# Counting edges per bucket: column sums of one-hots, moved from VectorE to TensorE

## The chip, the cores and the metric

The kernel runs on one core of a Trainium2 chip. The metric is the device time of one execution in microseconds (us). A core has five engines that run their own instruction streams and meet at semaphores: TensorE (PE in the rows; its weight loads are shown apart as PEld), VectorE (DVE), ScalarE (ACT), GpSimd (POOL) and SyncE (SP), which here only issues transfers.

## The reference

Four layers follow one another on 8192 rows of 128 numbers, each added to its input: a dense attention over an adjacency matrix, an expert layer whose gates come from a graph attention over 524288 edges, a second dense attention, and a routed expert layer. The change lies in the preparation of the edges for the second layer, which needs, for each destination node, sums over the edges that lead to it:

```python
src = jnp.concatenate([edge_index[0], loops])
dst = jnp.concatenate([edge_index[1], loops])
e = jax.nn.leaky_relu(a_src[src] + a_dst[dst], negative_slope=0.2)
e_max = jax.ops.segment_max(e, dst, num_segments=M)
ee = jnp.exp(e - e_max[dst])
denom = jax.ops.segment_sum(ee, dst, num_segments=M)
alpha = ee / (denom[dst] + 1e-16)
agg = jax.ops.segment_sum(h[src] * alpha[:, :, None], dst, num_segments=M)
```

## The kernel before

Edges lie as 128 partitions by CE = 4096 columns. Edges into the last row with a source beyond it ("same") are only counted; the others whose both ends lie in the 8192 rows are "plain" and get sorted into NF = 64 buckets, one for each tile of 128 destination nodes.

The function sort_and_project has two phases. In "pack" VectorE squeezes the plain edges of each partition to the left, so that only some hundred columns are left, and writes to ctl how many groups of GB = 64 columns the fullest partition needs. In "bucket" each plain edge gets its place: its rank among all edges of its bucket. Each phase ends in a barrier of all engines.

The bucket phase, by engine, in program order:

- GpSimd makes tile_no (the bucket numbers 0 to 63, each repeated 64 times) and keep, clears a column of recs, and then stores packed pieces of the adjacency.
- VectorE first **counts**: for each group it compares tile_no with the group's bucket numbers partB (L788, a one-hot tile of 64 buckets by 64 columns), sums the one-hot over its columns (L793, into some) and adds that to held (L794). Then it signals held_ok and waits for base_ok. It copies BASE into column 0 of D1 (L800), takes the largest total (L801) and derives from it the number of rounds and of fills (L802 to L807). Then it **places**: for each group a one-hot, a scan along the columns, a product, a reduction over the buckets (L818), eight small steps and a signal to SyncE to store the group's part of the plan. At last it makes one-hots for the same edges (L920, L921) and copies the histogram (L836).
- TensorE packs the adjacency: for every tile of 128 rows by 1024 words that ScalarE loads, eight matmuls with 8 columns (L857). Tiles come in units of four, in a ring of eight buffers (NRB); FIRST = 5 units are packed before the counts are wanted, the other 25 after them. Between the two stand two fp32 matmuls on held (L863, L864): one with tri (how many edges of a bucket lie in earlier partitions) and one with ones (how many the bucket has in all). After the packing TensorE counts the same edges in pairs of strided one-hots (L870, closed by L872).
- ScalarE issues the loads of the adjacency tiles, each when a buffer has been eaten, and copies each packed unit out of PSUM (L750).
- SyncE loads H, waits for rounds_ok, fills rec with empty records, and stores each placed group of the plan.

The order on each engine is the order of its program; nothing is planned by cost.

Of the kernel before, what the change touches and what calls it, by code (L numbers as in the profile page):

```python
# [8 lines left out]
ALU = mybir.AluOpType  # L9
ACT = mybir.ActivationFunctionType  # L10
AX = mybir.AxisListType
F32 = mybir.dt.float32
BF16 = mybir.dt.bfloat16
# [5 lines left out]
P = 128  # L19
BANK = 512  # L20
# [219 lines left out]
def sort_and_project(nc, ident, edge_index, N, rec, plan, ctl, repeat, classes,  # L240
# [4 lines left out]
    CE = E // P  # L245
    NF = N // P
    GB = 64
# [10 lines left out]
    with Phase(nc, "sort") as ph:  # L258
# [3 lines left out]
        tri = ph.sbuf("tri", [P, P])  # L262
        ones = ph.sbuf("ones", [P, P])
# [4 lines left out]
        with Phase(nc, "pack") as pk:  # L268
# [6 lines left out]
            plain = pk.sbuf("plain", [P, CE], BF16)  # L275
            S = [pk.sbuf(f"S{k}", [P, CE], I32) for k in range(2)]
            t1 = pk.sbuf("t1", [P, CE])
            scr = pk.sbuf("scr", [P, 6])
            cntc = pk.sbuf("cntc", [P, 2])
            top2 = pk.sbuf("top2", [P, 1])  # L280
            scri = pk.sbuf("scri", [P, 4], I32)
# [26 lines left out]
            groups = [(q, 0, EARLY) for q in range(BLOCKS)] + [(0, EARLY, 3), (0, EARLY + 3, KB - EARLY - 3)]  # L308
# [39 lines left out]
            with nc.Block() as block:  # L348
# [55 lines left out]
                def _(dve):  # L404
# [132 lines left out]
                    step(nc.vector.tensor_reduce(scr[0:1, 5:6], PS[0:1, 2 * P:3 * P], AX.X, ALU.max))  # L537
                    groups_of(0, scr[0:1, 4:5], 2 * GC, 2 * GC + 1.0)
                    groups_of(2, scr[0:1, 4:5], GB)
                    groups_of(3, scr[0:1, 5:6], GC)  # L540
                    step(nc.vector.tensor_scalar(ctl[0:1, 3:4], ctl[0:1, 3:4], float(HELD // GC), 1.0, ALU.subtract, ALU.max))

# [136 lines left out]
        with Phase(nc, "bucket") as pb:  # L679
# [4 lines left out]
            keep = pb.sbuf("keep", [P, NF, GB + 1], BF16)  # L684
            D1 = pb.sbuf("D1", [P, NF, GB + 1])
            ST = pb.sbuf("ST", [P, NF, GB + 1])
            hot = ST[:].rearrange("p t c -> p (t c)").bitcast(BF16)[:, 0:NF * GB].rearrange("p (t c) -> p t c", t=NF)
            some = pb.sbuf("some", [P, NF])
            held = pb.sbuf("held", [P, NF])
            most = pb.sbuf("most", [P, 2])  # L690
            mosti = pb.sbuf("mosti", [P, 2], I32)
            rank = pb.sbuf("rank", [P, GB])
# [12 lines left out]
            pk_out = [pb.sem(f"pk_out{k}") for k in range(2)]  # L705
            HC = CE // 2
            HISTC = pb.psum("histc", [P, BANK])
            BASE = pb.psum("base", [P, 2, BANK])
            same_hot, same_counted, same_ok, zero_ok, made, cleared, empty_ok, dve_step, held_ok, base_ok, rounds_ok, placed = pb.sems(
                "same_hot", "same_counted", "same_ok", "zero_ok", "made", "cleared", "empty_ok", "dve_step", "held_ok", "base_ok", "rounds_ok", "placed")  # L710
            fill_out, plan_out, pool_step, rows_in, passed, classes_out = pb.sems(
                "fill_out", "plan_out", "pool_step", "rows_in", "passed", "classes_out")
            COUNT, EDGE = 3, 13
            slots = rec.rearrange("(p c) k -> p c k", p=P)
            with nc.Block() as block:
                @block.gpsimd
# [61 lines left out]
                @block.vector  # L778
                def _(dve):
                    same_groups = dve.value_load(ctl[0:1, 3:4], min_val=1, max_val=(HC - HELD) // GC)  # L780
                    groups = dve.value_load(ctl[0:1, 2:3], min_val=1, max_val=CE // GB)
                    nc.vector.memset(zero[:], 0.0).then_inc(zero_ok, 1)
                    step = LoopSteps(dve, dve_step)
                    step.now(nc.vector.memset(held[:], 0.0))
                    dve.wait_ge(made, 2)

                    def hots(out, i):
                        return nc.vector.tensor_tensor(out, tile_no[:], partB[:, bass.ds(i * GB, GB)].unsqueeze(1).to_broadcast([P, NF, GB]), ALU.is_equal)  # L788

                    with dve.Fori(0, groups) as i:  # L790
                        step = LoopSteps(dve, dve_step, 1 + i * COUNT)
                        step.now(hots(hot, i))
                        step.now(nc.vector.tensor_reduce(some[:], hot, AX.X, ALU.add))  # L793
                        step.now(nc.vector.tensor_tensor(held[:], held[:], some[:], ALU.add))  # L794
                        assert step.n == COUNT
                    dve.sem_inc(held_ok, 1)
                    first = dve.snap(groups * COUNT + 1)
                    step = LoopSteps(dve, dve_step, first)
                    dve.wait_ge(base_ok, 1)
                    step.now(nc.vector.tensor_copy(D1[:, :, 0], BASE[:, 0, 0:NF]))  # L800
                    step.now(nc.vector.tensor_reduce(most[:, 0:1], BASE[:, 1, 0:NF], AX.X, ALU.max))  # L801
                    step.now(nc.vector.tensor_scalar(most[:, 1:2], most[:, 0:1], float(P * LEAST), float(P - 1), ALU.max, ALU.add))  # L802
                    step.now(nc.vector.tensor_copy(mosti[:, 0:1], most[:, 1:2]))
                    step.now(nc.vector.tensor_scalar(ctl[0:1, 1:2], mosti[0:1, 0:1], LOGP, None, ALU.arith_shift_right))
                    step.now(nc.vector.tensor_scalar(mosti[0:1, 1:2], ctl[0:1, 1:2], float(FILL - 1), None, ALU.add))
                    step.now(nc.vector.tensor_scalar(ctl[0:1, 4:5], mosti[0:1, 1:2], FILL.bit_length() - 1, None, ALU.arith_shift_right))
                    step.now(nc.vector.tensor_scalar(ctl[0:1, 5:6], ctl[0:1, 1:2], -1.0, None, ALU.add))  # L807
                    dve.sem_inc(rounds_ok, 1)
                    dve.wait_ge(cleared, 1)
                    with dve.Fori(0, groups) as i:  # L810
                        step = LoopSteps(dve, dve_step, first + 8 + i * EDGE)
                        cols = bass.ds(i * GB, GB)
                        step.now(hots(D1[:, :, 1:GB + 1], i))
                        step.now(nc.vector.tensor_tensor_scan(ST[:].rearrange("p t c -> p (t c)"), keep[:].rearrange("p t c -> p (t c)"),
                                                              D1[:].rearrange("p t c -> p (t c)"), 0.0, ALU.mult, ALU.add))
                        step.now(nc.vector.tensor_copy(D1[:, :, 0], ST[:, :, GB]))
                        step.now(nc.vector.tensor_tensor(ST[:, :, 1:GB + 1], ST[:, :, 1:GB + 1], D1[:, :, 1:GB + 1], ALU.mult))
                        step.now(nc.vector.tensor_reduce(rank[:], ST[:, :, 1:GB + 1].rearrange("p t c -> p c t"), AX.X, ALU.add))  # L818
                        step.now(nc.vector.tensor_scalar(ri[:, 0, :], rank[:], -1.0, 0.0, ALU.add, ALU.max))
                        dve.sem_inc(passed, 1)  # L820
                        step.now(nc.vector.tensor_copy(ri[:, 1, :], partB[:, cols]))
                        step.now(nc.vector.tensor_scalar(ri[:, 2, :], ri[:, 0, :], P - 1, LOGC, ALU.bitwise_and, ALU.logical_shift_left))
                        step.now(nc.vector.tensor_scalar(ri[:, 3, :], ri[:, 0, :], LOGP, LOGF, ALU.logical_shift_right, ALU.logical_shift_left))
                        step.now(nc.vector.tensor_tensor(ri[:, 2, :], ri[:, 2, :], ri[:, 3, :], ALU.bitwise_or))
                        step.now(nc.vector.tensor_scalar(ri[:, 3, :], ri[:, 1, :], LOGF, 28, ALU.logical_shift_right, ALU.logical_shift_left))
                        step.now(nc.vector.tensor_tensor(ri[:, 2, :], ri[:, 2, :], ri[:, 1, :], ALU.bitwise_or))
                        step.now(nc.vector.tensor_tensor(recs[:, cols, 2], ri[:, 2, :], ri[:, 3, :], ALU.bitwise_or))
                        dve.sem_inc(placed, 1)
                        assert step.n == EDGE
                    with dve.Fori(0, same_groups) as i:  # L830
                        for b in range(2):
                            dve.wait_ge(same_counted, 2 * i + b + 1)
                            cols = bass.ds(i * GC + b * HC + HELD, GC)
                            one_hots_across(nc, OFC[b], OPC[b], value, offC[:, cols], partC[:, cols], NF, GC)[1].then_inc(same_hot, 1)
                    dve.wait_ge(same_ok, 1)
                    nc.vector.tensor_copy(repeat[:], HISTC[:, 0:NF]).then_inc(held_ok, 1)  # L836
                    dve.wait_ge(held_ok, 2)
                    dve.wait_ge(rows_in, 16)
                    nc.vector.memset(H[:, :, D - 1], 1.0).then_inc(held_ok, 1)
                    dve.wait_ge(held_ok, 3)  # L840

                @block.tensor
                def _(pe):
# [4 lines left out]
                    def pack(some):  # L848
                        for u in some:
                            if u >= 2:  # L850
                                pe.wait_ge(emptied, u - 1)
                            for t in range(RT):
# [5 lines left out]
                                                           start=True, stop=True)  # L858
                                ins.then_inc(eaten, 1)

                    pack(range(FIRST))
                    pe.wait_ge(held_ok, 1)
                    nc.tensor.matmul(BASE[:, 0, 0:NF], tri[:], held[:], start=True, stop=True)  # L863
                    nc.tensor.matmul(BASE[:, 1, 0:NF], ones[:], held[:], start=True, stop=True).then_inc(base_ok, 1)  # L864
                    pack(range(FIRST, UNITS))
                    with pe.Fori(0, same_groups) as i:
                        for b in range(2):
# [2127 lines left out]
```

## Time and profile before

| | us |
|---|---|
| median of 3 runs (3690.57 to 3706.22) | 3698.13 |
| the profiled execution: its time | 3702.64 |
| the profiled execution: its span, first to last instruction | 3701.0 |
| TensorE busy, matmuls (16350) | 2732.4 |
| TensorE busy, weight loads (16350) | 1679.7 |
| VectorE busy | 2369.3 |
| ScalarE busy | 1369.6 |
| GpSimd busy | 1087.6 |

The busy times are sums over the whole span, over stages with different limits. The span is what the rows below count time in, from its start; the profiled execution takes 1.6 us more than its span. The bucket phase lies between about 411 and 606 us.

### The profile page before, as it was taken

To read this page: it belongs to the slowest core of one execution; us is meant where nothing else is said; L and a number is where in the kernel's file an instruction comes from. 1 tells how busy PE (TensorE), PEld (TensorE's weight loads), DVE (VectorE), ACT (ScalarE), POOL (GpSimd) and SP (SyncE) were. 2 spreads that over 40 slices of the span, in tenths; PEclk is the share of its full clock that TensorE was granted. 3 is DMA by queue.
4 is the path that set the end of the run, shared out by engine and by line. 5 is a ranking of instruction groups with operands and counts; after the bars stand their busy time and mean duration, and the time that the engine had idled before them with its cause. 6 is when DMAs were issued, how large, how long until landed. Compare 5 with 4: busy or idle time off the path is not lost. (4 is left out here: it accounts for less than half of the span.)

```text
span 3701.0 us, 55128 instructions
## 1 busy us (share of the span) xinstructions
PE 2732.4 (74%) x16350; PEld 1679.7 (45%) x16350; DVE 2369.3 (64%) x4532; ACT 1369.6 (37%) x2278; POOL 1087.6 (29%) x1035
## 2 busy tenths in 40 slices
PE   0442123999999999955888785246999999949994
PEld 0332122444444444424665564244655555526662
DVE  9999797787888878776444446794444444433333
ACT  5310100777777878753344341033000000012221
POOL 0000103777773000001655565000111111114442
PEclk9999999999999999975898895557999999969997
DMA  5999895554545445431111111342333333324446
GB/s 194 355 368 410 321 396 192 182 198 176 187 175 196 186 174 201 158 100 29 43 45 42 42 42 16 104 161 81 104 104 103 108 108 103 108 70 124 126 122 195
DMA packets 233854, 568.88 MB, mean 154 GB/s; under 512 B 52113, under 2 KB 93944, under 8 KB 225134
## 3 DMA queue, kind: packets, MB, share of 16 engines
q1 hardware_dynamic: 146006, 376.34, 29.7%
q10 hardware_dynamic: 56152, 163.80, 11.8%
q0 software_dynamic: 31552, 27.13, 3.3%
q8 instruction: 51, 0.84, 0.1%
q14 instruction: 93, 0.76, 0.1%
HBM read 443.12 MB, written 125.87 MB: 154 GB/s over the span
## 5 line engine op out<-in xcount | busy, mean ns | idle before, releaser
L1881 PE MATMUL at_out<-at_pt,top_H 128*128 128x512 f32 x2048 | 931.7, 601 | 34.8 <-ACT at_agg L1733 29.8
L1723 ACT ACTIVATE at_rl<-at_qrow,at_less,at_steep 128x512 f32<-128x512 f32 x1024 | 741.5, 804 | 89.6 <-DVE at_pt L1809 49.6
L1809 DVE SCALAR_TENSOR_TENSOR at_pt<-at_rl,at_turned 128x1024 f32<-128x1024 f32 x512 | 626.2, 1223 | 157.2 <-PE at_out L1881 80.7
L2098 PE MATMUL at_out<-at_parts,at_a 128*128 128x387 bf16 x4096 | 689.3, 328 | 28.8 <-DVE at_parts L2171 15.7
L1881 PEld LDWEIGHTS at_out<-at_pt,top_H 128*128 128x128 f32 x2048 | 373.0, 190 | 439.2 <-issue 396.6
L2098 PEld LDWEIGHTS at_out<-at_parts,at_a 128*128 128x128 fp8e4 x4096 | 399.4, 98 | 305.6 <-issue 36.8
L903 POOL DMA_INDIRECT rec<-at_part x304 | 384.2, 1264 | 104.9 <-issue 93.2
L1161 POOL DMA_INDIRECT edges_GT<-tab,gat_RC x320 | 339.9, 1062 | 237.0 <-DMA edges_GT<-tab,gat_RC 153.0
L2046 POOL DMA_INDIRECT slots<-at_Y,at_dest x128 | 123.2, 962 | 650.7 <-DVEq L2276 614.6
L648 PE MATMUL pack_bp<-top_weights,sort_recs 128*128 128x8 bf16 x1696 | 76.0, 170 | 233.4 <-DMA sort_recs<-in_adj_dram 233.4
L2549 PE MATMUL ex_hp<-ex_XS,ex_WB 128*128 128x512 f32 (+1 forms) x472 | 217.7, 598 | 1.9 <-DMA ex_WB<-wts 1.9
L2655 POOL DMA_INDIRECT y<-ex_YS,ex_to x156 | 153.3, 983 | 200.3 <-DVE ex_YS L2636 158.8
L2133 ACT ACTIVATE at_small<-at_small 128x4 f32<-128x4 f32 x16 | 3.3, 205 | 517.9 <-DVEq L2229 517.9
L2615 DVE TENSOR_TENSOR ex_HH<-ex_SU,ex_hp 128x512 f32<-128x512 f32 (+1 forms) x118 | 80.9, 686 | 162.8 <-ACT ex_SU L2593 133.3
L648 PEld LDWEIGHTS pack_bp<-top_weights,sort_recs 128*128 128x128 fp8e4 x1696 | 62.0, 106 | 248.7 <-DMA sort_recs<-in_adj_dram 140.8
L1142 POOL IOTA edges_node_no<- 128x128 f32 x1 | 0.2, 237 | 579.3 <-POOLq L63 579.3
L1408 PE MATMUL edges_hp<-top_H,edges_up 128*128 x256 | 150.2, 717 | 19.9 <-issue 17.3
L2593 ACT ACTIVATE ex_SU<-ex_hp 128x512 f32<-128x512 f32 (+1 forms) x118 | 70.3, 596 | 235.7 <-PE ex_hp L2549 192.0
L1800 DVE TENSOR_SCALAR at_turned<-at_packed 128x512 uint16<-128x512 uint16 x520 | 147.9, 286 | 0.0
L1419 PEld LDWEIGHTS edges_yp<-edges_down,f_YB 128*128 128x128 f32 x1024 | 139.5, 211 | 18.6 <-issue 15.9
L1455 PE MATMUL edges_lk<-f_YB 128*128 128x64 bf16 x928 | 119.4, 301 | 30.0 <-DVE f_YB L921 20.3
L857 PE MATMUL bucket_bp<-top_weights,bucket_raw 128*128 128x8 bf16 x960 | 43.9, 170 | 126.9 <-DMA bucket_raw<-in_adj_dram 126.9
(551 smaller groups left out, 3695.4 us busy)
## 6 DMA issues: line engine op xcount, KB each, us to landing
sort_recs<-in_adj_dram SPq DMA_DIRECT2D x212, 512.0 KB, 8.9
at_adj<-in_adj_dram SPq DMA_DIRECT2D x192, 512.0 KB
adjT<-at_turned ACTq DMA_DIRECT2D x64, 1024.0 KB
at_a<-adjT SPq DMA_DIRECT2D x128, 512.0 KB
bucket_raw<-in_adj_dram ACTq DMA_DIRECT2D x120, 512.0 KB, 10.2
ex_WB<-wts SPq DMA_DIRECT2D x42, 533.0 KB
y<-f_YB ACTq DMA_DIRECT2D x64, 256.0 KB
f_YB<-y SPq DMA_DIRECT2D x16, 1024.0 KB, 10.4
```

Of the source, the lines that this page charges most:

```text
L648: ins = nc.tensor.matmul(BP[:, u % 2, o:o + WORDS // 4], raw_bits[s % NR][:, k * P:(k + 1) * P, 0], weights[:], start=True, stop=True)
L903: pool.indirect_dma_start(rec, bass.IndirectOffsetOnAxis(ap=part[h][:, c, 2:3], axis=0), part[h][:, c, 0:2], None, bounds_check=LAST, oob_ ...
L1161: pool.indirect_dma_start(GT[g][:, c, :], None, tab, bass.IndirectOffsetOnAxis(ap=RC[g][:, c, 1:2], axis=0)).then_inc(gt_in[g], 16)
L1408: nc.tensor.matmul(HP[:, k, :], up[:, e, k * P:(k + 1) * P], XT[:, bass.ds(slab[0] * GQ, GQ), :], start=True, stop=True).then_inc(h_ok, 1)
L1419: ins = nc.tensor.matmul(YP[:, q * D:(q + 1) * D], HH[e % 2][k][:, q * P:(q + 1) * P], down[:, e, k, :], start=False, stop=(q == GQ - 1 an ...
L1723: ins = nc.scalar.activation(RL[v % NBUF][:, k, :], qrow[:], ACT.Relu, bias=less[:], scale=steep[:, u:u + 1])
L1800: ins = nc.vector.tensor_scalar(planes[m % 2][:, :, :, b, :], PK[:, m * JP:(m + 1) * JP, :].rearrange("p j (t w) -> p j t w", t=RT), b, 0x ...
L1809: nc.vector.scalar_tensor_tensor(out=PT[v % NBUF][:], in0=RL[v % NBUF][:], scalar=1.0, in1=AT[v // VP % 2][:, 2 * (v % VP):2 * (v % VP) + ...
L1881: ins = nc.tensor.matmul(OUT[:], H[:, u, :], PT[v % NBUF][:, k, :], start=(u == 0), stop=(u == T - 1))
L2098: ins = nc.tensor.matmul(OUT[:, g, x, 0:3 * D1], ones[c % NBUF][:, j, x * P:(x + 1) * P], parts[:, u].rearrange("p k d -> p (k d)"), start ...
L2549: ins = nc.tensor.matmul(HP[0:n, k, s, :], WB[b][:, w:w + n], XS[b][:], start=True, stop=True)
L2655: pool.indirect_dma_start(y, bass.IndirectOffsetOnAxis(ap=to[b][:, q:q + 1], axis=0), YS[b][:, q, :], None, bounds_check=2 * N - 1, oob_is ...
```

## The change

The one-hots stay on VectorE, but nothing is summed there. VectorE writes them into two tiles, hot[0] and hot[1], in turns, and TensorE multiplies each of their 64 columns with one fixed bf16 matrix, ahead: tri with its column 0 set to one. All products add up in one PSUM bank, BASE. Partition 0 of BASE then holds the totals, the other partitions the counts of the partitions before them. Groups are counted in pairs, so ctl gets a seventh entry, the number of pairs. hot_ok tells TensorE that a one-hot is made, hot_used tells VectorE that one has been read; the loop of TensorE stands where the two fp32 matmuls stood. VectorE's column 0 of D1 is cleared in partition 0, and some, held and the second bank of BASE are gone.

```diff
-            scr = pk.sbuf("scr", [P, 6])
+            scr = pk.sbuf("scr", [P, 8])
...
                     groups_of(2, scr[0:1, 4:5], GB)
+                    groups_of(6, scr[0:1, 4:5], 2 * GB)
...
-            hot = ST[:].rearrange("p t c -> p (t c)").bitcast(BF16)[:, 0:NF * GB].rearrange("p (t c) -> p t c", t=NF)
-            some = pb.sbuf("some", [P, NF])
-            held = pb.sbuf("held", [P, NF])
+            flags = ST[:].rearrange("p t c -> p (t c)").bitcast(BF16)
+            hot = [flags[:, k * NF * GB:(k + 1) * NF * GB].rearrange("p (t c) -> p t c", t=NF) for k in range(2)]
+            ahead = pb.sbuf("ahead", [P, P], BF16)
...
-            BASE = pb.psum("base", [P, 2, BANK])
+            BASE = pb.psum("base", [P, BANK])
...
+                    pairs = dve.value_load(ctl[0:1, 6:7], min_val=1, max_val=CE // (2 * GB))
                     nc.vector.memset(zero[:], 0.0).then_inc(zero_ok, 1)
                     step = LoopSteps(dve, dve_step)
-                    step.now(nc.vector.memset(held[:], 0.0))
+                    step.now(nc.vector.tensor_copy(ahead[:], tri[:]))
+                    step.now(nc.vector.memset(ahead[:, 0:1], 1.0))
+                    dve.sem_inc(ahead_ok, 1)
                     dve.wait_ge(made, 2)
...
-                    with dve.Fori(0, groups) as i:
-                        step = LoopSteps(dve, dve_step, 1 + i * COUNT)
-                        step.now(hots(hot, i))
-                        step.now(nc.vector.tensor_reduce(some[:], hot, AX.X, ALU.add))
-                        step.now(nc.vector.tensor_tensor(held[:], held[:], some[:], ALU.add))
-                        assert step.n == COUNT
-                    dve.sem_inc(held_ok, 1)
-                    first = dve.snap(groups * COUNT + 1)
-                    step = LoopSteps(dve, dve_step, first)
+                    with dve.Fori(0, pairs) as i:
+                        for k in range(2):
+                            dve.wait_ge(hot_used, 2 * i + k + 1)
+                            dve.sem_inc(passed, 1)
+                            hots(hot[k], 2 * i + k).then_inc(hot_ok, 1)
+                    step = LoopSteps(dve, dve_step, COUNT)
                     dve.wait_ge(base_ok, 1)
-                    step.now(nc.vector.tensor_copy(D1[:, :, 0], BASE[:, 0, 0:NF]))
-                    step.now(nc.vector.tensor_reduce(most[:, 0:1], BASE[:, 1, 0:NF], AX.X, ALU.max))
+                    step.now(nc.vector.tensor_reduce(most[:, 0:1], BASE[:, 0:NF], AX.X, ALU.max))
+                    step.now(nc.vector.tensor_copy(D1[:, :, 0], BASE[:, 0:NF]))
+                    step.now(nc.vector.memset(D1[0:1, :, 0], 0.0))
...
+                    pe.sem_inc(hot_used, 2)
+                    pe.wait_ge(ahead_ok, 1)
                     pack(range(FIRST))
-                    pe.wait_ge(held_ok, 1)
-                    nc.tensor.matmul(BASE[:, 0, 0:NF], tri[:], held[:], start=True, stop=True)
-                    nc.tensor.matmul(BASE[:, 1, 0:NF], ones[:], held[:], start=True, stop=True).then_inc(base_ok, 1)
+                    pairs = pe.value_load(ctl[0:1, 6:7], min_val=1, max_val=CE // (2 * GB))
+                    nc.tensor.matmul(BASE[:, 0:NF], zero[:], zero[:, 0:NF], start=True, stop=False, skip_group_check=True)
+                    with pe.Fori(0, pairs) as i:
+                        for k in range(2):
+                            pe.wait_ge(hot_ok, 2 * i + k + 1)
+                            pe.sem_inc(passed, 1)
+                            for c in range(GB):
+                                ins = nc.tensor.matmul(BASE[:, 0:NF], ahead[:], hot[k][:, :, c], start=False, stop=False, skip_group_check=True)
+                            ins.then_inc(hot_used, 1)
+                    nc.tensor.matmul(BASE[:, 0:NF], zero[:], zero[:, 0:NF], start=False, stop=True, skip_group_check=True).then_inc(base_ok, 1)
                     pack(range(FIRST, UNITS))
```

## Rows read from the trace of the kernel before

**Rows 1.** Windows over counting and placing: stretch, length, busy time of each engine.

```profile
core 0: us, PE busy (x) PEld busy (x) DVE busy (x) ACT busy (x) POOL busy (x), PEclk, DMA share, GB/s
...
420.20:457.20 37.00, 7.46 (x160) 5.84 (x160) 34.68 (x15) 1.86 (x5) 6.30 (x3) 1.00 1.01 404
...
460.30:600.80 140.50, 34.90 (x756) 27.48 (x752) 135.08 (x65) 9.30 (x25) 7.01 (x13) 1.00 0.93 363
```

**Rows 2.** Waits between 400 and 640: total us, times, longest.

```profile
PE bucket_histc L870 <- DVE bucket_OPC L921: 12.7, 1, 12.7
...
PE bucket_base L863 <- DVEq L796: 4.8, 1, 4.8
```

**Rows 3.** Timeline of the phase's start: start, us, instruction [idle before <-releaser].

```profile
404.16 5.64 ACT L620 COPY sort_recs<-pack_S 128x4096 int32<-128x4096 int32 x1
...
405.50 0.14 DVE L541 TENSOR_SCALAR top_ctl<-top_ctl 1x1 int32<-1x1 int32 x1
411.09 0.34 SPq L754 DMA_DIRECT2D top_H<-rows  x1
...
412.72 0.11 DVE L782 MEMSET bucket_zero<- 128x64 uint32 x1 [7.08 <-issue]
...
420.20 2.29 DVE L788 TENSOR_TENSOR bucket_ST<-bucket_tile_no,sort_partB 128x4096 bf16<-128x4096 bf16 x1 [7.29 <-POOL bucket_keep L724]
422.52 4.42 DVE L793 TENSOR_REDUCE bucket_some<-bucket_ST 128x64 f32<-128x4096 bf16 x1
...
427.66 2.29 DVE L788 TENSOR_TENSOR bucket_ST<-bucket_tile_no,sort_partB 128x4096 bf16<-128x4096 bf16 x1 [0.46 <-DVE bucket_held L794]
...
443.15 0.30 PEld L857 LDWEIGHTS bucket_bp<-top_weights,bucket_raw 128*128 128x128 fp8e4 x8 [2.84 <-issue]
...
452.05 0.38 PE L857 MATMUL bucket_bp<-top_weights,bucket_raw 128*128 128x8 bf16 x8 [0.91 <-DMA bucket_raw<-in_adj_dram]
...
457.70 0.64 PE L864 MATMUL bucket_base<-bucket_held,sort_ones 128*128 128x64 f32 x2
...
458.37 0.28 DVE L800 COPY bucket_D<-bucket_base 128x64 f32<-128x64 f32 x1 [1.42 <-PE bucket_base L864]
```

**Rows 4.** Timeline of the phase's end.

```profile
589.31 0.38 PE L857 MATMUL bucket_bp<-top_weights,bucket_raw 128*128 128x8 bf16 x8 [0.86 <-DMA bucket_raw<-in_adj_dram]
...
590.46 0.54 POOL L728 DMA_DIRECT2D packed_adj<-bucket_pkd  x1 [9.62 <-ACT bucket_pkd L750]
...
600.49 0.24 DVE L827 TENSOR_TENSOR sort_recs<-bucket_ri 128x64 int32 x1 [0.16 <-DVE bucket_ri L826]
...
604.65 0.23 DVE L836 COPY top_repeat<-bucket_histc 128x64 f32<-128x64 f32 x1 [1.34 <-PE bucket_histc L872]
...
606.18 0.34 SPq L1694 DMA_DIRECT2D at_packed<-packed_adj  x1
```

**Rows 5.** Groups on VectorE, 412 to 606: count | busy us, mean ns | idle.

```profile
L818 DVE TENSOR_REDUCE bucket_rank<-bucket_ST 128x64 f32<-128x4096 f32 x5 | 37.2, 7448 | 0.2
...
L793 DVE TENSOR_REDUCE bucket_some<-bucket_ST 128x64 f32<-128x4096 bf16 x5 | 22.1, 4420 | 0.2
```

**Rows 6.** Timeline of the self-edge matmuls, 603.9 to 605.

```profile
603.66 0.90 PE L870 MATMUL bucket_histc<-bucket_OFC,bucket_OPC 128*128 128x64 bf16 x6
...
604.27 0.12 PEld L872 LDWEIGHTS bucket_histc<-bucket_zero 128*128 128x128 bf16 x1
604.38 0.23 PE L872 MATMUL bucket_histc<-bucket_zero 128*128 128x64 bf16 x1
```

**Rows 7.** Timeline of a later stage: matmuls with adjoining moving columns.

```profile
1774.14 0.62 PE L1448 MATMUL edges_out<-edges_VP,edges_OH 128*128 128x60 bf16 x16
```

**Rows 8.** Groups on TensorE over the whole span, shapes apart.

```profile
L1455 PE MATMUL edges_lk<-f_YB 128*128 128x64 bf16 x928 | 119.4, 301 | 30.0 <-DVE f_YB L921 20.3 <-issue 9.7
...
L1448 PE MATMUL edges_out<-edges_VP,edges_OH 128*128 128x60 bf16 x320 | 14.3, 199 | 14.5 <-DVEq L1265 11.5 <-issue 3.0
```

**Rows 9.** The page's DMA issues: count, KB each, us to landing.

```profile
bucket_raw<-in_adj_dram ACTq DMA_DIRECT2D x120, 512.0 KB, 10.2
```

More of the change, by code:

```diff
@@ L707, in sort_and_project @@
             HISTC = pb.psum("histc", [P, BANK])
-            BASE = pb.psum("base", [P, 2, BANK])
+            BASE = pb.psum("base", [P, BANK])
             same_hot, same_counted, same_ok, zero_ok, made, cleared, empty_ok, dve_step, held_ok, base_ok, rounds_ok, placed = pb.sems(
                 "same_hot", "same_counted", "same_ok", "zero_ok", "made", "cleared", "empty_ok", "dve_step", "held_ok", "base_ok", "rounds_ok", "placed")
-            fill_out, plan_out, pool_step, rows_in, passed, classes_out = pb.sems(
-                "fill_out", "plan_out", "pool_step", "rows_in", "passed", "classes_out")
-            COUNT, EDGE = 3, 13
+            fill_out, plan_out, pool_step, rows_in, passed, classes_out, hot_ok, hot_used, ahead_ok = pb.sems(
+                "fill_out", "plan_out", "pool_step", "rows_in", "passed", "classes_out", "hot_ok", "hot_used", "ahead_ok")
+            COUNT, EDGE = 2, 13
             slots = rec.rearrange("(p c) k -> p c k", p=P)
@@ L810, in _ @@
                     with dve.Fori(0, groups) as i:
-                        step = LoopSteps(dve, dve_step, first + 8 + i * EDGE)
+                        step = LoopSteps(dve, dve_step, COUNT + 9 + i * EDGE)
                         cols = bass.ds(i * GB, GB)
@@ L836, in _ @@
                     nc.vector.tensor_copy(repeat[:], HISTC[:, 0:NF]).then_inc(held_ok, 1)
-                    dve.wait_ge(held_ok, 2)
+                    dve.wait_ge(held_ok, 1)
                     dve.wait_ge(rows_in, 16)
                     nc.vector.memset(H[:, :, D - 1], 1.0).then_inc(held_ok, 1)
-                    dve.wait_ge(held_ok, 3)
+                    dve.wait_ge(held_ok, 2)
                 @block.tensor
```

## Prediction

> **What bounds the kernel now.** The page names the big groups of the kernel, none of which the change touches, and its chain of waits reaches back only into the last stage. So the stage of the change has to be read by itself: windows over the bucket phase, then waits, then the timeline at its two ends.
>
> The windows [rows 1] cut the phase where VectorE changes its work. While it counts (420.2 to 457.2) VectorE is busy 34.68 of 37.0 us; while it places edges (460.3 to 600.8) 135.08 of 140.5. In both the DMA engines are also full (share 1.01 and 0.93), because the adjacency stream for TensorE's packing runs there, while TensorE itself is busy 7.46 us in the counting, at a granted clock of 1.00, the 2.4 GHz level, which I keep. Two things could therefore end the phase, and the timeline of the end [rows 4] says which: packing's last matmuls start at 589.31 and its last store is issued at 590.46, but VectorE writes its last records at 600.49 and leaves at about 605.1, and the next phase's first transfer follows at 606.18. VectorE's chain sets the end, with the packing some 12 us in front of it. The waits agree [rows 2]: TensorE waits 12.7 us for VectorE before the last counting matmuls.
>
> A phase ends in a barrier of all engines, so what moves this end moves all that follows, one for one; I see nothing later that could take it up.
>
> Now the start [rows 3]. VectorE counts five groups from 420.20, a turn every 7.46 us. TensorE packs 5 units meanwhile, as tiles land, is through with them at 452.05 + 0.38 = 452.4, and waits 4.8 us [rows 2] for the counts. Its two prefix matmuls release VectorE at 458.37.
>
> **The change, part by part.**
>
> *Taken from VectorE:* five sums of 4.42 us [rows 5] and their small adds. That is over 22 us of busy time on the engine that sets the end, but it is worth only what brings 458.37 forward.
>
> *Which work now comes last before that point.* The new counting stands on TensorE behind the same first 5 units of packing, and those follow the DMA stream, which nothing here quickens. VectorE makes two one-hots by about 424.8 (420.20 plus two of 2.29 [rows 3]) and then has no free buffer; it waits until TensorE, from 452.4 on, has used the first. So VectorE's 28 us of idle time take the place of its sums, and the time until 458.37 is no longer filled with counting done beside the packing. The saving is lost whole unless TensorE counts all groups in the 6 us that are left.
>
> *How many matmuls.* The five turns of placing [rows 5] are the groups of 64 columns, so the fullest row has between 257 and 320 plain edges; rounded up to pairs of 128 columns that is 3 pairs, 6 groups, 6 x 64 = 384 matmuls of 64 columns, each with a weight load of its own: the table ahead has as many loads as matmuls.
>
> *What one costs.* The moving operand takes one column in 64 of a bf16 tile: a step of 128 bytes. No row shows that step; the nearest bound it. From below: 16 matmuls with 60 adjoining moving columns span 0.62 us [rows 7], a single one takes about 0.20 [rows 8], so they start every (0.62 - 0.20)/15 = 0.028 us. From above: the counting of self edges at the phase's end, 64 moving columns with a step of 16 bytes, six in 0.90 us, with 0.30 for a single one [rows 8], so one every (0.90 - 0.30)/5 = 0.12 us [rows 6]. There the weights are strided too, so which operand is it? The last one answers: the weight load behind it (L872) reads an adjoining tile, and still the next matmul starts only at 604.38, 0.11 us after that load began together with the previous matmul [rows 6]. It was the moving operand that took 0.11 to 0.12 us, or 1.8 ns a column. VectorE gives the same figure from another side: its sum over adjoining elements takes 4420 ns for 4096, the one that steps by 260 bytes 7448 ns [rows 5], again 1.8 ns an element; so the price does not seem to grow between 16 and 260 bytes. I take 0.120 us, by the row whose moving operand is nearest: 384 x 0.120 = 46.1 us.
>
> The Trainium skill, "SBUF — State Buffer", under "Door 1: The DMA port swizzle", says that SBUF is read in lines of 16 bytes and each access that crosses to a new line pays; this is the rule that speaks against the change, since here every column lies in a line of its own. The trace agrees for a step of one line [rows 6], and by the rule 128 bytes would cost the same: the sum is unchanged.
>
> *Around it on TensorE.* A register load: two of them and the start of VectorE's program lie between 411.09 and 412.72 [rows 3], so about 0.8 us. First count at 452.4 + 0.8 = 453.2; end of counting 499.3. The closing matmul takes 0.23 [rows 6], and VectorE follows 0.04 behind such a one (604.65 against 604.38 + 0.23 [rows 4, 6]). Three turns of the loop: VectorE's own turn costs 0.46 [rows 3]; TensorE's run ahead of queued matmuls, so between 0 and 1.4; I take 0.4. VectorE starts again at 500.0 instead of 458.37: +41.6. One more small step, clearing a column of D1, replaces nothing: +0.2. **Together +41.8 us.**
>
> *Covered parts.* VectorE's refill of a one-hot, 2.29 plus a hand-over of about 0.5, lies under TensorE's 7.7 us for a group; without that cover (at 0.028, 1.8 us a group) it would set the pace at about 2.5 us. The bf16 copy of tri, the extra register load and the removed clearing stand before VectorE's wait for GpSimd's tile, which ended at 420.2 after 7.3 us [rows 3]; without that cover under 1 us. Three small steps for the pairs, some 0.5 us by the like at 0.14, lie in the earlier phase under ScalarE's copy of the records, which ends 4 us after VectorE [rows 3]. The two fp32 prefix matmuls, which end at 457.70 + 0.64 = 458.34 [rows 3], go and are counted in the difference.
>
> *What queues behind TensorE.* Packing from the sixth unit on, so the ring of 8 tiles, ScalarE's loads, its copies and GpSimd's stores. Eight tiles of 512 KB [rows 9] at the 404 GB/s of [rows 1] last 10.4 us, so the stream, which runs on through today's 5 us, dries up at about 463 and stands until 500. Packing took from 458 to 590.5 before; from 500.0 it ends at about 632, some 4 later with an empty ring: 636. VectorE's chain ends at 605.1 + 41.8 = 646.9. So the packing stays hidden, with 11 us to spare; the fill of rec and the plan stores on SP's queue move with VectorE and still land inside.
>
> The sum: the profiled execution took 3702.6 us (span 3701.0); 3702.6 + 41.8 = 3744.4. It lies 4.5 above the median of the runs, so the prediction is 3698.1 + 41.8 = **3740**.
>
> **Rivals.**
>
> *The step costs nothing (not slower).* If 64 columns at 128 bytes stream at 0.028 us, a group is 1.8 us, VectorE's refill paces four groups at 2.5, and base_ok comes at about 467.4 (first refill at 457.4, three more turns of 2.5, the last group and the close): +9 us, 3707, which is within 0.5% (about 18.5 us, what a measurement here tells from no change). It decides below 0.060 us a matmul. For it speaks [rows 7], against it [rows 6]. 7 in 100. The Trainium skill, "TensorE: Matmul & The Clock Gate", "Back-to-back issue gap", gives N/2.4 + 2.5 ns, 29 ns for 64 columns, without regard to steps, and would make it this case; the trace agrees for adjoining columns [rows 7] and not for stepped ones [rows 6].
>
> *Half way.* One column in about 0.9 ns, 0.058 us a matmul: 22.3 us of counting, +18 us, 3716. For it: the two strided operands may have shared the price [rows 6]; against it the L872 row there. 10 in 100.
>
> *The step costs more than 16 bytes do.* At twice the price, 0.24 us, counting takes 92 us: +88, 3786; at one and a half times it is 3763. No row of TensorE excludes it, VectorE's 260 bytes speak against it [rows 5]. 10 in 100.
>
> *Code is late.* A stall of 2.84 us at TensorE that nothing in the profile explains stands at 443.15 [rows 3], while the DMA engines were full. Three turns of such a stall add 8.5: 3749. It is inside my main case, as is the packing ending last (beyond 647, it needs 11 us more than I give it).
>
> *Faster.* The change would have to bring the release before 458.37. Six groups at even 0.028 us take 10.8 us from 453.2 on, so only a shorter placing loop could do it, and that is unchanged: 3 in 100, 3690.
>
> **How the numbers follow.** Main case, 70 in 100: pitch between 0.115 us (44.2 us of counting) and 0.129 (49.5; 928 matmuls of the same kind in 119.4 us, over stretches of other work [rows 8]), loop and code 0 to 8.5: +39 to +54, so 3737 to 3752. With the half-way case at the low end and the smaller half of the dearer one at the high end, the range is 3713 to 3760 and leaves out about 17 in 100. Slower by over 0.5%: main, dearer and a good half of half-way, 0.86; same 0.11; faster 0.03.
>
> **What would show it.** In the changed profile: VectorE idle from about 425 to 455, released by TensorE; 384 matmuls of the new line starting every 0.12 us; the first step after base_ok at 500; a hole in the adjacency stream from about 463 to 500; the placing loop of the same 140 us; the phase's end near 647, again on VectorE. Wrong would be: a pitch under 0.06, TensorE counting before its 5 units are packed, or the packing ending after VectorE.

## The result and the profile after

The changed kernel takes 3741.8 us (median of 4 runs, 3729.6 to 3767.6). The kernel before takes 3696.0 beside it (4 runs). The ratio is 1.0119 [1.0096, 1.0142], or +44 us with an interval of +35 to +53. The prediction was 3740, in a range of 3713 to 3760. The profiled execution has a span of 3743.5 us, where 3701.0 + 41.8 = 3742.8 would follow from the forecast; this near hit is partly luck, as the next rows show.

The timeline of the changed kernel, from the phase's first transfer to that of the next phase (start, us, instruction [idle before <-releaser]); the first row is the end of the phase before; the rows after it and the last ones answer to [rows 3, 4]:

```profile
407.44 5.60 ACT L621 COPY sort_recs<-pack_S 128x4096 int32<-128x4096 int32 x1
...
414.33 0.34 SPq L755 DMA_DIRECT2D top_H<-rows  x1
...
416.60 6.17 DVE L786 CAST bucket_ahead<-sort_tri 128x128 bf16<-128x128 f32 x1
...
423.58 4.50 DVE L792 TENSOR_TENSOR bucket_ST<-bucket_tile_no,sort_partB 128x4096 bf16<-128x4096 bf16 x2 [0.68 <-POOL bucket_keep L725]
...
455.27 0.38 PE L859 MATMUL bucket_bp<-top_weights,bucket_raw 128*128 128x8 bf16 x8 [0.90 <-DMA bucket_raw<-in_adj_dram]
...
455.95 0.23 PE L867 MATMUL bucket_base<-bucket_zero 128*128 128x64 bf16 x1 [0.30 <-issue]
456.25 42.64 PEld L873 LDWEIGHTS bucket_base<-bucket_ST,bucket_ahead 128*128 128x128 bf16 x384 [0.20 <-issue]
...
463.80 2.29 DVE L792 TENSOR_TENSOR bucket_ST<-bucket_tile_no,sort_partB 128x4096 bf16<-128x4096 bf16 x1 [35.72 <-PE bucket_base L873]
470.92 2.29 DVE L792 TENSOR_TENSOR bucket_ST<-bucket_tile_no,sort_partB 128x4096 bf16<-128x4096 bf16 x1 [4.83 <-PE bucket_base L873]
...
499.03 1.87 PE L859 MATMUL bucket_bp<-top_weights,bucket_raw 128*128 128x8 bf16 x64
499.25 0.23 DVE L801 TENSOR_REDUCE bucket_most<-bucket_base 128x1 f32<-128x64 f32 x1 [11.79 <-PE bucket_base L875]
...
501.44 4.43 DVE L792 TENSOR_TENSOR bucket_D<-bucket_tile_no,sort_partB 128x4096 f32<-128x4096 bf16 x1 [0.35 <-DVE top_ctl L809]
...
630.89 0.54 POOL L729 DMA_DIRECT2D packed_adj<-bucket_pkd  x1 [9.59 <-ACT bucket_pkd L751]
...
645.76 0.23 DVE L838 COPY top_repeat<-bucket_histc 128x64 f32<-128x64 f32 x1 [1.36 <-PE bucket_histc L883]
...
647.33 0.35 SPq L1705 DMA_DIRECT2D at_packed<-packed_adj  x1
```

In this execution the phase began at 414.33 instead of 411.09, because ScalarE's copy of the records in the phase before ended at 413.04 instead of 404.16 + 5.64 = 409.80. That is not the change: e4 and e8 below have the same phase before, and there it began at 411.15 and 411.65; all other profiles lie between 408.2 and 411.7. So the kernels are compared from their phase's first transfer. From there, VectorE was released after 458.37 - 411.09 = 47.3 us before and after 499.25 - 414.33 = 84.9 now: +37.6, where the forecast had +41.6. The whole phase, first transfer to first transfer, grew from 195.1 to 233.0 us, +37.9. With the 3.2 of the late start and 1.3 in the stages that follow, this makes the span's 42.5, to rounding.

The idle times in brackets tell the rest. VectorE makes two one-hots and then stands 35.72 us for TensorE, which finishes its five units at 455.65, only then counts, and frees the first one-hot after its 64 columns. The refills of the one-hots lie 7.12 us apart: 64 columns at 0.111 us, and nothing to spare for the loop.

Windows over counting beside packing, counting alone, placing, and two parts of the counting (answers to [rows 1]):

```profile
core 0: us, PE busy (x) PEld busy (x) DVE busy (x) ACT busy (x) POOL busy (x), PEclk, DMA share, GB/s
420.20:452.40 32.20, 6.31 (x136) 4.99 (x136) 7.13 (x4) 1.49 (x4) 9.55 (x5) 1.00 1.01 409
452.40:502.00 49.60, 45.98 (x474) 45.54 (x474) 11.21 (x14) 0.74 (x2) 0.00 (x0) 1.00 0.26 100
502.00:642.00 140.00, 34.14 (x736) 26.97 (x736) 134.51 (x65) 8.93 (x24) 7.02 (x13) 1.00 0.93 361
...
461.00:469.00 8.00, 8.00 (x74) 8.00 (x73) 2.29 (x1) 0.00 (x0) 0.00 (x0) 1.00 0.33 130
...
469.50:476.00 6.50, 6.50 (x61) 6.50 (x60) 2.29 (x1) 0.00 (x0) 0.00 (x0) 1.00 0.00 0
```

VectorE had 34.68 busy us of 37 while it counted [rows 1]; now 7.13 of 32.2. The saving is there and buys nothing. In the second row TensorE is busy nearly throughout, and in the last one the adjacency stream stands (DMA share 0.00). What follows the release is as long as it was: from there to VectorE's last copy 604.65 - 458.37 = 146.3 us before, 645.76 - 499.25 = 146.5 now.

### The profile page after: what moved, and what is told of

Read it like the earlier page. It is cut to its first block and busy times, and to the rows that moved or that the text cites. A ratio compares the mean times of both kernels' runs of the same rounds, so it can differ in the third digit from the quotient of the medians.

```text
span 3743.5 us, 55900 instructions
## 1 busy us (share of the span) xinstructions
PE 2776.5 (74%) x16732; PEld 1720.4 (46%) x16732; DVE 2355.4 (63%) x4528; ACT 1371.0 (37%) x2278; POOL 1097.2 (29%) x1035
```

## Experiments

The theory: the change costs two things, the *place* of the counting behind five packing units, and the *step* of the moving operand, 128 bytes from column to column, which makes TensorE pay for a 16-byte line per column. The rivals: the pitch of 0.111 us belongs to matmul and weight load as such, whatever the step; 128 bytes cost something that 16 do not; or the counting isn't what sets the end. The runs were made on two other occasions, with medians of the kernel before of 3679.2 and 3677.6 us; the stages after this phase are some 19 to 34 us shorter there than in the profile of before, in every kernel, so spans can't be set against those of the changed kernel, as several expectations do. Releases and phase lengths are compared instead, both from the phase's first transfer, with the 47.3 and 195.1 of the one profile of before, and times by ratio alone. A ratio without an interval is that of a single run.

| run | one column every | pitch, us | release | phase | ratio to before |
|---|---|---|---|---|---|
| before | | | 47.3 | 195.1 | 1 |
| changed kernel | 128 B | 0.111 | 84.9 | 233.0 | 1.0119 [1.0096, 1.0142] |
| e1_step16 | 16 B | 0.116 | 86.6 | 234.8 | 1.0106 |
| e6_step8_clean | 8 B | 0.060 | 65.3 | 213.4 | 1.0059 |
| e2_step4 | 4 B | 0.043, then 0.030 | 60.1 | 208.2 | 1.0041 |
| e5_step4_clean | 4 B | 0.048, then 0.030 | 63.4 | 211.5 | 1.0045 [1.0026, 1.0064] |
| e3_adjoining | 2 B | 0.030 to 0.048 | 85.7 | 233.9 | 1.0083 [1.0067, 1.0100] |
| e4_count_first | 128 B | 0.111 | 54.7 | 216.9 | 1.0046 [1.0031, 1.0061] |
| e7_step4_first | 4 B | 0.056, 0.046, then 0.030 | 27.9 | 190.3 | 0.9988 [0.9975, 1.0000] |
| e8_twice | 128 B, 768 matmuls | 0.110 | 126.6 | 274.7 | 1.0194 |

Release and phase length hang together: the phase ends 147.8 us after the release before, 148.1 to 148.2 in the changed kernel and in e1, e2, e3, e5, e6 and e8, and 162.2 and 162.4 in e4 and e7, where packing starts only after the counting.

**e1_step16, e2_step4, e3_adjoining: the layout of the one-hot.** Within a one-hot W columns of a bucket adjoin, so the step is 2W bytes: W = 8, 2, 1. GpSimd makes a second tile of bucket numbers in this order.

```diff
-hot = [... .rearrange("p (t c) -> p t c", t=NF) ...]
+hot = [... .rearrange("p (g t w) -> p g t w", t=NF, w=W) ...]
...
+nc.gpsimd.iota(tile_w, pattern=[[0, GB // W], [1, NF], [0, W]], ...)
...
-nc.tensor.matmul(BASE[:, 0:NF], ahead[:], hot[k][:, :, c], ...)
+nc.tensor.matmul(BASE[:, 0:NF], ahead[:], hot[k][:, c // W, :, c % W], ...)
```

> The changed kernel with the one-hots laid out so that TensorE's moving columns step by 16 bytes instead of 128; all else the same. If each column pays for a line of 16 bytes of its own, whatever the step beyond that, the 384 matmuls start every 0.11 us as before and the counting takes 43 us. If the price grows with the step, they start clearly faster, below 0.09 us, and the counting takes under 35 us. Span within 5 us of the changed kernel by the first, about 10 us or more shorter by the second.

> The same with a step of 4 bytes, so that four columns lie in one line of 16 bytes. By the line rule the price falls by more than half, to 0.03 to 0.05 us a matmul and 13 to 20 us of counting. If any step between columns costs (the rival), it stays at 0.11 us and 43 us. If the weight load sets the pace, 0.11 us too.

> The same with adjoining columns. By the theory that the moving operand's step is the price, a group takes TensorE 1.8 to 2 us, VectorE's refill of 2.3 us plus the hand-over then sets the pace, the counting takes 13 to 15 us instead of 43, VectorE is released near 470 and the time is about 29 us under the changed kernel's, near 3713, still 10 to 15 us over the kernel before, since the counting stands behind the first five units. If 384 matmuls with their weight loads are the price whatever the layout, no change against the changed kernel. If the hole in the adjacency stream were the cost, also most of it would go, but then packing would end the phase, not VectorE.

The counting matmuls of e1_step16 (least/median/most ns, stretch, tile):

```profile
L879 PE MATMUL bucket_base<-bucket_ST,bucket_ahead x384: 276/294/296, 452.7 to 497.1; 128*128 128x64 bf16 x192
```

With 16 bytes the 384 matmuls start 0.116 us apart: all that 128 bytes cost is there at one line a column. The phase is 1.8 us longer than the changed kernel's, within the 5 expected of the span. With 4 bytes the pitch fell to 0.043 and then 0.030, and the counting to 16 us, as expected. e3 missed: its matmuls are as fast, but its release hardly moved. Its rows tell why (timeline of e3_adjoining):

```profile
408.22 40.34 POOL L721 IOTA bucket_D<- 128x4096 bf16 x1 [14.30 <-POOLq L63]
...
410.45 38.19 DVE L790 CAST bucket_ahead<-sort_tri 128x128 bf16<-128x128 f32 x1
...
454.03 4.42 DVE L803 TENSOR_TENSOR bucket_ST<-bucket_D,sort_partB 128x4096 bf16<-128x4096 bf16 x1 [5.26 <-POOL bucket_keep L727]
```

GpSimd needed 40.34 us for the new tile, VectorE's copy of tri into ahead lasted until that tile was done, and TensorE waits for ahead before it packs; packing began at 448.9, and the first one-hot was made only at 454. So the counting took 24 us instead of 42.6, but began 19.6 us later, taken from the phase's start; its pace was set by the one-hots, 4.42 us each in this layout. The timed ratio gives +31 us (25 to 37) against before, somewhat less than the phase's +38.8; in the profiled execution the phase began 2.9 us earlier than before's. e2 has the same fault at half the size (GpSimd's tile 22.88 us, the cast 20.72). Both bear on the pitch, not on the time.

**e5_step4_clean, e6_step8_clean: the same without GpSimd's tile.** The bucket numbers are read from a table of the phase before (value), and ahead is made at that phase's end; VectorE's wait for GpSimd moves behind the counting. W = 2 and 4.

```diff
+ahead = ph.sbuf("ahead", [P, P], BF16)
...
+bucket_no = value[:, 0:NF, 0:W].unsqueeze(1).to_broadcast([P, GB // W, NF, W])
...
-dve.wait_ge(made, 2)
...
+dve.wait_ge(made, 2)
...
-pe.wait_ge(ahead_ok, 1)
```

> A step of 4 bytes again, with what disturbed the two runs before it taken out: the bucket numbers come from the small tile value, repeated by the access pattern, so GpSimd makes no second tile; the fixed matrix is cast at the end of the earlier phase; VectorE no longer waits for GpSimd before it counts. The counting still stands behind five units. By the theory (price of the step, and place) TensorE counts in 14 to 16 us instead of 43, VectorE is released some 57 us after the phase's first transfer (47.3 before, 84.9 in the changed kernel), and the time is 8 to 12 us over the kernel before, 27 to 30 under the changed one. If the place costs nothing, it comes out at or under the kernel before.

> The same with a step of 8 bytes, two columns to a line of 16 bytes. If the price is one of lines, a matmul starts every 0.055 to 0.06 us or, where two hits on a line are enough to hide it, every 0.03 us as with 4 bytes; a price for any step above 4 bytes would give 0.11 us.

The counting matmuls and loads by tile (least/median/most ns, stretch, tile), first e6_step8_clean, then e5_step4_clean after its first two groups:

```profile
L874 PEld LDWEIGHTS bucket_base<-bucket_ST,sort_ahead x384: 105/115/122, 453.2 to 476.1; 128*128 128x128 bf16 x192
L874 PE MATMUL bucket_base<-bucket_ST,sort_ahead x384: 218/238/241, 453.2 to 476.2; 128*128 128x64 bf16 x192
```

```profile
L874 PEld LDWEIGHTS bucket_base<-bucket_ST,sort_ahead x256: 95/96/98, 461.4 to 474.6; 128*128 128x128 bf16 x128
L874 PE MATMUL bucket_base<-bucket_ST,sort_ahead x256: 189/191/194, 461.5 to 474.6; 128*128 128x64 bf16 x128
```

Two columns to a line instead of one, and the pitch halves (23.05 us for 384, 0.060); two were not enough to hide the price, four were. The weight load reads the same adjoining tile in all these runs, and the pitch still went from 0.111 to 0.060 and 0.030 with the moving operand's step; so the load is not what sets the pitch, and the first rival falls. (The record of the load itself shortens too, from a median of 124 ns in the changed kernel to 115 and 96.) The release of e6 came 18.0 us after that of before, and the half-way rival of the prediction, priced at 0.058 us a matmul, had +18.

In e5 TensorE is no longer the slow one. Its timeline, third and fourth group:

```profile
461.45 2.06 PE L874 MATMUL bucket_base<-bucket_ST,sort_ahead 128*128 128x64 bf16 x64 [1.71 <-DVE bucket_ST L799]
465.19 2.06 PE L874 MATMUL bucket_base<-bucket_ST,sort_ahead 128*128 128x64 bf16 x64 [1.68 <-DVE bucket_ST L799]
```

TensorE works 2.06 us and waits 1.7 for VectorE, whose one-hot takes 3.7 us when it reads the bucket numbers as pairs from value, instead of 2.29; read in fours from value (e6), or in pairs from a ready tile (e2), it took 2.29. That, and the slow start of the first two groups (0.048 us a matmul), is why e5's release missed its expectation (63.4 after the start, some 57 expected; 21 us of counting, 14 to 16 expected), and why the phase still ended 16.4 us later than before, where 8 to 12 were expected. A cheap step alone does not save the change.

**e4_count_first: the place alone.** Nothing is packed ahead of the counting.

```diff
-FIRST = 5
+FIRST = 0
```

> The changed kernel with its counting loop ahead of all packing on TensorE instead of behind five units; the step stays 128 bytes. If the place is half of the cost, the counting (again 43 us) ends near 470 instead of 499 and VectorE's chain ends near 617 instead of 646; but packing starts only then, and by the stream's rate it ends near 626 and the phase near 630: 16 us under the changed kernel, 25 over the kernel before, with packing as the end. The rival, that VectorE still ends the phase, gives 29 us under the changed kernel.

The pitch is the same, the release comes 30 us earlier than in the changed kernel, and the phase is 16.1 us shorter, as expected. The rest of the 30 went to another engine. The end of its timeline:

```profile
608.24 0.25 DVE L829 TENSOR_TENSOR sort_recs<-bucket_ri 128x64 int32 x1 [0.15 <-DVE bucket_ri L828]
...
624.97 0.23 DVE L838 COPY top_repeat<-bucket_histc 128x64 f32<-128x64 f32 x1 [13.92 <-PE bucket_histc L883]
```

VectorE wrote its last records at 608.24 and then waited 13.92 us for TensorE, which was packing: the 5 units that had been packed before the counting now come after it. In this kernel the packing ends the phase. Against before, 25 us were expected, reckoned from the forecast's +41.8; by the phase it is +21.8, and the timed ratio gives +17 (11 to 22).

**e7_step4_first: both.** e5 with FIRST = 0.

> The kernel of the step of 4 bytes with the counting ahead of all packing. TensorE counts while the first tiles are still on their way and the ring of eight fills, so the stream has no hole; VectorE is released about 20 us after the phase's first transfer and its chain would end near 578 on the clock of the profile before; packing, at its old pace, ends near 590 and the phase near 594 instead of 606: 10 to 12 us under the kernel before, 0.3 per cent, with the packing as the end. The rival, that delayed packing pushes the stream back, gives no gain or a loss of up to 10 us.

Windows of e7_step4_first over counting and over the rest of the phase, then the end of its timeline:

```profile
core 0: us, PE busy (x) PEld busy (x) DVE busy (x) ACT busy (x) POOL busy (x), PEclk, DMA share, GB/s
414.00:439.00 25.00, 14.80 (x383) 14.11 (x383) 22.67 (x6) 0.00 (x0) 11.73 (x6) 1.00 0.82 336
440.00:597.00 157.00, 42.90 (x936) 34.10 (x934) 138.13 (x76) 11.18 (x30) 7.60 (x14) 0.51 1.00 393
```

```profile
597.21 0.54 POOL L733 DMA_DIRECT2D packed_adj<-bucket_pkd  x1 [9.83 <-ACT bucket_pkd L755]
598.65 0.22 DVE L840 COPY top_repeat<-bucket_histc 128x64 f32<-128x64 f32 x1 [13.96 <-PE bucket_histc L884]
```

The release is now 19.4 us earlier than before, 27.9 us after the phase's first transfer where 20 were expected: six one-hots at some 3.8 us from value set the pace. The phase is 4.8 us shorter (10 to 12 expected), and the time 0.12% less, with an interval that ends at 1.0000: on the fast side, and less than a measurement of this kernel can well tell. Where the other 14.6 us went is in the same rows: VectorE waits 13.96 us for the packing again, and the DMA engines are full for 157 us (share 1.00). The stream stood in the last 4 us before 440 (share 0.00 from 436 on), its ring of eight tiles full and nothing packed; from the release to the last store packing took 157.9 us, as it did in e4. What a still earlier release could gain can be estimated from these rows: here the phase ends 4.5 us after the last store is issued (597.21, 601.69), and before that store was issued at 590.46, so with the packing where it lay before the phase could end near 595 instead of 606.18, some 11 us earlier, whoever does the counting.

**e8_twice: the price doubled.** Every counting matmul is preceded by one with the zero matrix on the same columns, which adds nothing to the counts.

```diff
+nc.tensor.matmul(BASE[:, 0:NF], zero[:], hot[k][:, :, c], ...)
 ins = nc.tensor.matmul(BASE[:, 0:NF], ahead[:], hot[k][:, :, c], ...)
```

> The changed kernel with each of the 384 matmuls preceded by one with a matrix of zeros on the same moving columns, which adds nothing to the sums. If TensorE's counting lies on the path in full, VectorE is released 42 to 43 us later and the span grows by as much over the changed kernel's, with VectorE still the end. If the hole in the stream set the end, the growth would be the same but the last packing store would come after VectorE's last records; if part of the counting is hidden, the growth is smaller.

Every second one of the counting matmuls of e8_twice, those with ahead:

```profile
L874 PE MATMUL bucket_base<-bucket_ST,bucket_ahead x384: 287/287/288, 453.3 to 537.8; 128*128 128x64 bf16 x192
```

768 matmuls took 84.6 us, 0.110 each; the release came 41.7 us later than in the changed kernel, and the phase is longer by the same 41.7, with VectorE still the end (last packing store at 670.18, VectorE's last copy at 684.75). The counting is on the path that sets the end, one for one; the third rival falls.

## Why the prediction was right, point by point

- *VectorE's chain ends the phase, the packing before it.* So it was: last store at 630.89, VectorE's last copy at 645.76. e8 shows the 1:1. Taken from the phase's start the last store came some 8 us before the 636 forecast: 4 because the count ended earlier, and 4 because the term "an empty ring" was wrong. The stream stood because the ring was full, and at 499.03 TensorE packed eight waiting tiles in one go (64 matmuls in 1.87 us); from the release to the last store packing took 131.6 us, 132.1 before.
- *The counting stands behind five packing units, and the saving on VectorE is lost whole.* Taken from the phase's start, the fifth unit ends at the same time as before (455.65 - 3.24 = 452.41; forecast 452.4). e4 and e7 show the place as a cause of its own: with it alone mended the release comes 30 us earlier, with the step alone (e5) 21.6.
- *384 matmuls, each paying for a 16-byte line per column.* The count was exact and the mechanism was right: 16 bytes cost as much as 128, 8 bytes half, 4 bytes about a quarter of it. So the rivals "half way" and "the step costs more than 16 bytes do" fall too. The size was off: 0.111 instead of 0.120, which is 384 x 0.009 = 3.5 us. The prediction took (0.90 - 0.30)/5 from six matmuls with two strided operands; the better row was its own L872 one, 0.11 us [rows 6]. VectorE's 1.8 ns an element, which the prediction took as a sign from another side, stays a likeness of two numbers that no run ties together; e1 is what shows that the price does not grow from 16 to 128 bytes. By the Trainium skill, "SBUF — State Buffer", "Door 1: The DMA port swizzle", each access that crosses to a new 16-byte line pays; the four steps from 128 to 4 bytes agree with it, but for a 16-byte step that is 4% dearer than 128 bytes, which stays open.
- *Register load 0.8, loop 0.4.* Both too dear: 0.60 us lie between the end of the last packing matmul (455.65) and the first counting load (456.25), and the refills come 7.12 us apart, which is the 64 matmuls alone. With the pitch these 0.2 and 0.4 us make up the 4 us between +41.6 and +37.6.
- *Code is late.* The loop shows no such stall: all four refills lie 7.12 us apart. The 2.84 us at 443.15 that were read as unexplained have a releaser in the row of the matmul that goes with that load, a transfer:

```profile
443.18 0.35 PE L857 MATMUL bucket_bp<-top_weights,bucket_raw 128*128 128x8 bf16 x8 [2.79 <-DMA bucket_raw<-in_adj_dram]
```

- *The total.* The phase grew by 37.9, not 41.8. The profiled execution's late start and longer tail, 4.6 us together, filled the gap; that is luck. The start has nothing to do with the change, and the 1.3 us of the tail lie in stages that it does not touch. The timed runs' interval, +35 to +53, holds both figures, and it is too wide to tell them apart.
- *Covered parts.* The refills lie under TensorE's groups, as forecast. The bf16 copy of tri was priced under 1 us and took 6.17; it was still covered, since TensorE's fifth unit did not move. Had GpSimd worked longer, it would have set the start of packing, as in e2 and e3.
- *The rival "the step costs nothing".* Its pitch is real, for other columns: 0.030 us at 2 and 4 bytes. The Trainium skill, "TensorE: Matmul & The Clock Gate", "Back-to-back issue gap", gives N/2.4 + 2.5 ns for a matmul by itself and says that this is too low for short matmuls in a stream with weight loads; for 64 columns it makes an estimate of 29 ns. e5's later groups, with a weight load for every matmul, agree with it as it stands (0.030); at 16 bytes and more it is short by a factor of nearly four. The forecast of +9 assumed one-hots of 2.29 us. e2 has them, and there the release comes 16.2 us after the zero matmul; behind a fifth unit at its old place that would be some +10.6, an estimate from e2 and the rows of before. In e5, whose one-hots take 3.7, it was +16.
- *A hole in the stream, at about 463 to 500.* Shown by the windows: DMA share 0.33, then 0.00, until the packing starts again at 499.03.

## What to carry to other kernels

Work taken off the engine that sets the end is worth only what it brings forward the next hand-over: ask behind what the new worker's program queues it, here five packing units that came with a transfer stream. Look at the step of a moving operand before the number of matmuls: here a bf16 column in a 16-byte line of its own cost nearly four times an adjoining one (0.111 against 0.030 us for 64), and four to a line would have been enough; but price the engine that has to write that layout too. When both are mended, the next bound (here the adjacency stream) decides whether anything is left to win.

## What was unexpected in the hardware

- **VectorE's cast waits out GpSimd.** The 128x128 copy from fp32 to bf16 took 0.23 us in the phase before, with GpSimd idle (e5, at 405.93), and 6.17, 9.74, 20.72 and 38.19 us when it was begun while GpSimd wrote its tiles (the changed kernel, e1, e2, e3). Each time it ended within 0.1 us of the end of a GpSimd instruction: of the iota in e2 and e3, of the clearing of keep that follows it in the changed kernel and e1. The one-hots took 2.29 us beside GpSimd's clearing of recs. What in the cast makes the difference was not tried.
- **GpSimd's iota pays for short runs.** 128x4096 bf16 numbers took 3.86 us in runs of 64 equal ones (e5), 7.42 in runs of 8 (e1), 22.88 of 2 (e2), 40.34 of 1 (e3).
- **Two pitches at one granted clock.** At 4 bytes the first groups of counting ran at 0.043 to 0.056 us a matmul, the later ones at 0.030, while the granted clock read 1.00, the 2.4 GHz level, in both; matmuls at 8 bytes and more, at 0.060 us and over, show no such start. Full DMA engines are not the reason: e7's third and fourth groups ran at 0.030 with a DMA share of 1.03 and 1.04. Left open.
- **The granted clock after counting.** The placing stage has the same packing on TensorE in every kernel, but not the same clock. In before, the changed kernel, e1, e4 and e8 it stayed at 1.00. In e2, e3, e5, e6 and e7, all with a counting pitch of 0.060 us or less, it was 0.50 over 500 to 600, the 1.2 GHz level. Gaps in the counting are not what sets them apart: in e6 TensorE counted 23.90 of 24.0 us and the clock fell, while before it was busy 7.46 of 37 us and kept 1.00. Why is open. The packing did not lose by it: from the release to the last store it took 157.9 us in e4 at 1.00 and in e7 at 0.51.
